# A four-layer graph network in one kernel: the work at the edges between its layers in another order

## The reference

```python
# layer 0
qk = h @ Wqk; q, k = split(qk); v = h @ Wv
w = inv_scale * mask * sum(q * (adj @ (k * mask)), -1)
x = x + softmax(w, axis=1)[:, :, None] * v
# layer 1
query, keyt, value = h @ Wq.T + bq, h @ Wk.T + bk, h @ Wv.T + bv
weight = adj * exp(query @ keyt.T)
x = x + (weight / sum(weight, 2)) @ value
# layer 2: 8 heads of 64
q, k, v = proj(Wq, bq), proj(Wk, bk), proj(Wv, bv)
attn = softmax((q @ k.T) * SCALE * (adj + adj))
x = x + (attn @ v) @ Wo.T + bo
# layer 3: 3 hops
Xw = h @ Wv + bv
e = leaky_relu((Xw @ aw[:d])[:, None, :] + (Xw @ aw[d:])[:, :, None] + ab, 0.2)
T = adj * exp(e) / (sum(adj * exp(e), -1) + 1e-12)
H = h @ Wk[0] + bk[0] + (T @ h) @ Wk[1] + bk[1] + (T @ T @ h) @ Wk[2] + bk[2]
x = x + relu(H)
```

## Time and profile before

| | us |
|---|---|
| time of the kernel, median of 3 runs | 2273.91 (2278.74, 2273.74, 2273.91) |
| the profiled execution, its own time | 2279.19 |
| span of its instructions in the trace | 2277.4 |
| PE busy | 2230.5 (98%) |
| DVE, ACT, POOL busy | 1317.8, 780.9, 722.9 |
| TensorE clock granted, mean | 0.994 of full speed |

### The profile page before, as it was taken

The page is one execution under the profiler, slowest core; times in us unless marked ns, Lnnn a source line. Parts: engine busy times, 40 slices in busy tenths (PEclk is TensorE's granted clock), DMA queues, the critical chain, the costliest instruction groups (busy, mean ns, idle before and its releaser), DMA issues.

```text
span 2277.4 us, 39277 instructions
## 1 busy us (share of the span) xinstructions
PE 2230.5 (98%) x15788; PEld 1767.0 (78%) x15788; DVE 1317.8 (58%) x2643; ACT 780.9 (34%) x1393; POOL 722.9 (32%) x927
## 2 busy tenths in 40 slices
PE   8999999999999999999999999999899999999998
PEld 4788878887887877888888888888677777777776
DVE  3565655656555566455565555564775757575752
ACT  3433333333223233333232333333343434343432
POOL 2433433343334323223332223332341313132320
PEclk9999999999999999999999999999999999999999
DMA  6333333333333343322333323334344242425231
GB/s 204 79 80 99 101 103 84 93 93 84 95 96 107 99 130 108 105 84 80 94 102 98 103 80 83 100 93 110 109 123 127 71 124 68 127 69 128 71 106 37
DMA packets 185687, 224.74 MB, mean 99 GB/s; under 512 B 69408, under 2 KB 85792, under 8 KB 185504
## 3 DMA queue, kind: packets, MB, share of 16 engines
q1 hardware_dynamic: 178832, 212.78, 34.0%
q10 hardware_dynamic: 6672, 9.45, 1.7%
HBM read 88.91 MB, written 50.37 MB: 61 GB/s over the span
## 4 chain that ended last, share of the span: by engine, by line
PE 78%; DVE 8%; SPq 5%; DMA 5%; POOL 1%; issue 1%; ACT 1%; DVEq 0%; ACTq 0%; POOLq 0%
PE bank L316 40%; PE bank L306 29%; SPq L951 5%; DVE junk L933 3%; PE bank L332 3%; DMA x<-mid 2%; PE bank L502 1%; PE bank L567 1%; PE bank L472 1%; PE bank L367 1%; DVE hs L635 1%; DVE stA L610 1%; DMA hGA<-hs 1%; DMA si<-stB 0%; DVE yt L933 0%
## 5 line engine op out<-in xcount | busy, mean ns | idle before, releaser
L316 PE MATMUL bank<-w_hi,h3T_hi 128*128 128x512 f32 x768 | 306.5, 399 | 1.8 <-ACT Z L958 1.8
L316 PE MATMUL bank<-w_lo,h3T_hi 128*128 128x512 f32 x768 | 300.7, 392 | 0.0
L316 PE MATMUL bank<-w_hi,h3T_lo 128*128 128x512 f32 x768 | 300.5, 391 | 0.0
L972 ACT ACTIVATE hn<-x,stA 128x512 f32<-128x512 f32 x192 | 140.7, 804 | 259.8 <-POOL stA L1208 253.9
L1203 POOL TENSOR_SCALAR stA<-stA 128x4 f32<-128x4 f32 x48 | 11.5, 240 | 672.7 <-DVE stA L612 672.5
L610 DVE BATCH_NORM_STATS2 stA<-x 128x6 f32<-128x512 f32 x192 | 128.3, 668 | 160.4 <-DMA x<-mid 151.2
L316 PEld LDWEIGHTS bank<-w_hi,h3T_hi 128*128 128x128 f32 x768 | 144.8, 189 | 56.6 <-issue 25.2
L958 ACT ACTIVATE Z<-bank 64x512 f32<-64x512 f32 x256 | 151.9, 593 | 83.0 <-PE bank L316 67.1
L316 PEld LDWEIGHTS bank<-w_hi,h3T_lo 128*128 128x128 f32 x768 | 145.0, 189 | 30.9
L316 PEld LDWEIGHTS bank<-w_lo,h3T_hi 128*128 128x128 f32 x768 | 144.8, 189 | 29.2
L1216 POOL TENSOR_TENSOR h1T_lo<-hGB,h1T_hi 128x512 fp32r<-128x512 f32 x64 | 81.6, 1304 | 199.2 <-ACT h1T_hi L958 199.2
(11 more groups left out here) (197 smaller groups left out, 5670.7 us busy)
## 6 DMA issues: line engine op xcount, KB each, us to landing
hGA<-hs SPq DMA_DIRECT2D x760, 64.0 KB, 2.0
mid<-x SPq DMA_DIRECT2D x32, 1024.0 KB, 4.5
x<-mid SPq DMA_DIRECT2D x32, 1024.0 KB, 5.9
hGB<-hs SPq DMA_DIRECT2D x256, 64.0 KB, 2.0
x<-in_x SPq DMA_DIRECT2D x15, 1024.0 KB, 5.8
out<-x SPq DMA_DIRECT2D x15, 1024.0 KB, 8.9
blk<-in_adj SPq DMA_DIRECT2D x128, 64.0 KB
PT<-hs SPq DMA_DIRECT2D x120, 64.0 KB, 2.0
```

Source lines behind the costliest of these rows:

```text
L316: ins = eng.matmul(b[:], h[l][:, k, ts], W[r][:, k, :], start=(k == 0 and i == 0), stop=(last and k == 3 and i == 2))
L972: eng.activation(h[t][:], xt[:, t, :], ACT.Relu, bias=st[:, t, 10:11], scale=st[:, t, 9:10]).then_inc(done, 1)
```

## The change

The order of work is changed at four places, and adj is read in another layout:

- **Start.** Layer 0's first operands, the two halves of Wqk, come in four quarters of each instead of two, with a semaphore each, and the first group of x is loaded by SP behind the first two quarters; before, ACT's queue issued it.
- **Layers 0/1 to layer 2.** q2(0) is computed right behind `l01_pv(14)`, ahead of `g1(15)`; ACT splits Wq2 and evicts QQ(0) in that turn. The whole chain of group 1 of layer 2 (statistics, scale, norm, transposes, gather) also goes into that turn; on SP it stands ahead of the load of Wv2.
- **Layer 2 to layer 3.** The row-sum instructions of group 0 (`l3_sums(0)`) go from the last turn with on = true to the one behind it, the transposes of layer 3's group 0 behind the context's lo part; the hi and lo parts of h3T(0) follow.
- **Layer 3.** `l3_rowsum(g)`, for g above 0, goes into group g's own turn, behind two z2 products (for g = 0 behind two z1 products) instead of the turn before; SP's transfers of the sums go behind the gather. The last group's y products and second hop are done by row halves (y 0, y 2, hop; y 1, y 3, hop).
- **Layout.** adj comes in three orders from the host (by rows, by columns, by heads). It needs one DMA for 4 (columns) or 2 for 4 (heads), in rows of 1 KB or more rather than 128 or 256 B, and DVE no longer transposes it (`adj_T`, one instruction per group and layer).

```diff
-                pe.wait_ge((d_qk0, d_qk1)[k // 2], 32)
+                pe.wait_ge(d_qk[k], 32)
...
+                if g == NG:
+                    l2_gemm_T("q2", 0, Wq2, a_q)
...
-                if on:
+                if on and g:
                     l2_gemm_T("q2", g, Wq2, a_q)
...
+            def l3_y(g, t):
+                gemm_open(("y", g, t), hT3[g % 2], t, W3[0], (v_y, 4 * g + (1, 3, 2, 4)[t]), False)
...
                 for t in range(4):
                     gemm(("z2", g, t), hT3[i], t, W3[2], (a_zh[0], 8 * g + 2 * t + 2))
-                    if g == 0 and t == 1:
-                        l3_rowsum(0)
+                    if g and t == 1:
+                        l3_rowsum(g)
                 pe.wait_ge(p_wlo, lo_pool["w1"])
                 for t in range(4):
                     gemm_open(("z1", g, t), hT3[i], t, W3[1], (a_zh[1], 8 * g + 2 * t + 2), False)
+                    if g == 0 and t == 1:
+                        l3_rowsum(0)
                 l3_hop(0, "z1", g)
                 pe.wait_ge(p_wlo, lo_pool["w0"])
-                for t in range(4):
-                    gemm_open(("y", g, t), hT3[i], t, W3[0], (v_y, 4 * g + (1, 3, 2, 4)[t]), False)
-                    if t == 1 + (g == 0) and g + 1 < NG:
-                        l3_rowsum(g + 1)
-                l3_hop(1, "y", g)
+                if g + 1 < NG:
+                    for t in range(4):
+                        l3_y(g, t)
+                    l3_hop(1, "y", g)
+                else:
+                    for r in range(2):
+                        l3_y(g, r)
+                        l3_y(g, 2 + r)
+                        l3_hop(1, "y", g, (r,))
...
                     features2_lo(0)
+                    stats_A(2, 1)
+                    split_in_place(Wk2, "k2")
+                    transposes(2, 1)
                 if on1:
-                    adj_T(0, g - 1)
-                    if g == NG:
...
                 if g == NG:
+                    l3_sums(dve, eng, 0, (0, 1))
                     l2_out(g - 2, 3)
-                stats_A(*(after2(g) if on else (3, 1)))
+                    l3_sums(dve, eng, 0, (2, 3))
+                    l2_out(g - 1, 0)
+                    l2_ctx(g - 1, 1)
+                    stats_A(3, 1)
+                    l2_out(g - 1, 1)
+                    transposes(3, 1)
+                    l3_alpha(0)
+                    l2_out(g - 1, 2)
+                    l3_sums(dve, eng, 1, (0, 1))
+                    l2_out(g - 1, 3)
+                    break
+                if g:
+                    stats_A(*after2(g))
                 if prev:
                     l2_out(g - 1, 0)
-                if on:
+                if on and 0 < g < NG - 1:
                     transposes(*after2(g))
                 if prev:
                     l2_ctx(g - 1, 1)
                 if g == NG - 1:
-                    l3_sums(dve, eng, 0, (0, 1))
+                    transposes(3, 0)
                 for u in range(2):
                     if prev:
                         for t in ((1,), (2,) if g == NG - 1 else (2, 3))[u]:
                             l2_out(g - 1, t)
-                    if on:
-                        l2_softmax(g, u)
-                    elif u == 0:
-                        transposes(3, 1)
-                        adj_T(3, 0)
-                        l3_alpha(0)
-                if not on:
-                    l3_sums(dve, eng, 1, (0, 1))
-                if on:
-                    dve.wait_ge(d_bv2, 16)
-                    if g == NG - 1:
-                        l3_sums(dve, eng, 0, (2, 3))
-                    for t in range(4):
-                        if t == 1:
-                            if g + 1 < NG:
-                                features2_lo(g + 1)
-                                l2_pT(g)
-                        dve.wait_ge(*bank.done(("v2", g, t)))
-                        if g:
-                            dve.wait_ge(*bank.done(("ctx", g - 1, 1, 1)))
-                        eng.tensor_tensor(VV[:, t, :], bank.of(("v2", g, t))[:], bv2, ALU.add).then_inc(v_vv, 1)
+                    l2_softmax(g, u)
+                dve.wait_ge(d_bv2, 16)
+                for t in range(4):
+                    if t == 1 and g + 1 < NG:
+                        features2_lo(g + 1)
+                        l2_pT(g)
+                    dve.wait_ge(*bank.done(("v2", g, t)))
+                    if g:
+                        dve.wait_ge(*bank.done(("ctx", g - 1, 1, 1)))
+                    eng.tensor_tensor(VV[:, t, :], bank.of(("v2", g, t))[:], bv2, ALU.add).then_inc(v_vv, 1)
...
                 if g == 0:
-                    l3_rowsum(0)
                     l3_sums(dve, eng, 1, (2, 3))
+                l3_rowsum(g)
                 if g + 2 < NG:
                     stats_A(3, g + 2)
                 if g + 1 < NG:
-                    adj_T(3, g + 1)
                     l3_alpha(g + 1)
                 if g + 2 < NG:
                     transposes(3, g + 2)
                     l3_sums(dve, eng, g + 2, range(4))
-                if g + 1 < NG:
-                    l3_rowsum(g + 1)
...
-            first = g == 0 and 0 in ts
...
+                    split_in_place(Wq2, d_q2)
                     act.wait_ge(*bank.done(("v1", NG - 2, 3)))
-                    features2_hi(1, NG - 1, hT[1], (0, 1, 2))
-                    split_in_place(Wq2, d_q2)
-                    features2_hi(1, NG - 1, hT[1], (3,))
+                    features2_hi(1, NG - 1, hT[1])
+                    l2_evict("q2", 0, QQ, 0, a_q)
...
-                if on:
+                if on and g:
...
-                if g == 0:
-                    norm_A(*after2(0))
...
-                if on and g:
+                if on and 0 < g < NG - 1:
                     norm_A(*after2(g))
                 if prev:
                     l2_ctx(g - 1, 1)
+                if g == NG - 1:
+                    norm_A(3, 0)
...
+                    l2_exp(g, 1)
                     if g == NG - 1:
                         split_in_place(W3[2], d_w2)
                         split_in_place(W3[1], d_w1)
...
-                elif on:
-                    act.wait_ge(v_dotA, 4)
-                    features2_hi(3, 0, hT3[0])
...
+                    act.wait_ge(v_cst, 1)
+                    features2_hi(3, 0, hT3[0])
...
-                    if g == 0 and t == 1:
-                        l3_T_other(0)
+                l3_T_other(g)
...
-                if g + 1 < NG:
-                    l3_T_other(g + 1)
...
                     scale_A(*((0, g + 1) if g + 1 < NG else (2, 0)))
+                else:
+                    scale_A(2, 1)
+                if on0:
...
+                    split_in_place(W3[2], "w2")
                     features_lo(3, 0, hT3[0], hGA, p_flo3)
-                    split_in_place(W3[2], "w2")
...
+                if g:
+                    l3_rowsum(g)
...
-                    l3_rowsum(g + 1)
...
-                eng.dma_start(abf[:, g % 2], adj_t[g]).then_inc(d_adj[g % 2], 16)
+                eng.dma_start(abf[:, g % 2].rearrange("p t n -> p (t n)"), adj_rows[g]).then_inc(d_adj[g % 2], 16)
...
+            for k in range(4):
+                if k == 2:
+                    load_x(0, x_v[0])
+                eng.dma_start(qT[:, k, :], qk_rows[:, k, :]).then_inc(d_qk[k], 16)
+                eng.dma_start(kTw[:, k, :], qk_rows[:, 4 + k, :]).then_inc(d_qk[k], 16)
...
+            load2(1)
+            gather(2, 1)
             for oc in range(4):
                 sp.wait_ge(*bank.done(("g1", NG - 1, oc)))
             eng.dma_start(Wv2["raw"][:], rows(L2_gnn_Wv)).then_inc(d_v2, 16)
...
-                if on:
+                if on and g:
                     gather(*after2(g))
                 if g == NG:
+                    load_blocks(3, 0)
+                    load3(2)
+                    sums_out3(0)
                     sums_in3(0)
                     gather(3, 1)
-                if g == NG - 1:
-                    sums_out3(0)
...
-            load3(2)
+            sums_out3(1)
+            sums_in3(1)
             for g in range(NG):
                 load_blocks(3, g + 1)
-                if g == 0:
-                    sums_out3(1)
-                sums_in3(g + 1)
-                sums_out3(g + 2)
                 gather(3, g + 2)
                 load3(g + 3)
...
```

120 lines of the change are left out of this document (54 added, 66 removed).

## The result

| | us |
|---|---|
| the kernel before, 5 runs | median 2277.93 (2273.74 to 2282.74) |
| the changed kernel, 5 runs | median 2291.38 (2290.01 to 2293.74) |
| ratio after to before, 95% interval | 1.0063 (1.0044 to 1.0081) |
| the profiled execution after, its own time and span | 2293.74 and 2291.9 (before: 2279.19 and 2277.4) |

A forecast was written before the change was run, and what follows sets the result against it. PE, busy 2230.5 of 2277.4 us, was taken as the bound, with some 47 us idle to change. The terms sum to +3.1: 2282.3 on the profiled execution, 2277.0 carried to the median; range 2264 to 2285 with the rivals.

The forecast's parts named there:

- What would show it: Signs listed for the later profile, such as PE waiting about 12 us on h2T_lo and some 4 us for cT_lo.
- Start, +1.2: Kernel start: g0 stays bound by x and its gather, gains 0.4 from adj, loses 1.6 to low clock; +1.2 us.
- q2(0) first, +7.4: Edge of layers 0/1 to 2: PE waits 11.8 us for h2T_lo(0) in place of 4.4; +7.4 us.
- Group 1's gather ahead of Wv2, +6.1: Same edge: the gather delays Wv2 and x2(15), so k2(0) waits 4.5 us plus 1.6 of clock; +6.1 us.
- Layers 2 to 3, -2.6: Edge of layers 2 and 3: z2(0) starts 4.8 us earlier, 2.2 are given back behind asum(0); -2.6 us.
- Layer 3 later, -7.2: Layer 3's later groups: three row-sum waits of 5.6 us go, with 1.6 of clock; -7.2 us.
- Tail, -1.8: Kernel end: by halves, only four DVE instructions remain behind PE's end instead of eight; -1.8 us.
- The layout, 0: adj's layout: DVE transposes and DMA issues go, all beside a PE that is the bound; 0 us.
- rival B: Slower, at layer 3's start: the list behind asum(0) is too long, -2.6 becomes +3.3, total 2283 us; chance 0.25.

The follow-up runs named there:

- e10: The changed kernel with group 0's x issued by ACT's queue at 0.7 us as before, Wqk still in quarters; ratio 1.0035 to the kernel before.
- e3: The changed kernel with h2T_lo(0) moved ahead of q2w_lo and x2(14) on DVE; ratio 1.0053 to the kernel before.
- e9: The changed kernel with h2T_lo(0) ahead of vf(14)'s first addition, q2w_lo between its second and third, Wv2 ahead of the gather; ratio 0.9967 to the kernel before.
- e2: The changed kernel with the load of Wv2 ahead of group 1's gather on SP; ratio 1.0031 to the kernel before.
- e7: The changed kernel with other orders of ACT and GpSimd in layer 3's first group only; ratio 1.0037 to the kernel before.
- e12: The changed kernel itself, unedited, measured again in a later session; ratio 1.0069 to the kernel before.
- e13: The kernel before with adj's new layout alone, every order as before; ratio 0.998 to the kernel before.
- e16: The kernel before with adj's new layout alone, profiled a second time; layer 3's 13 groups took 486.85 us.
- e6: The changed kernel with x loaded ahead of the gather on SP in layer 3's loop; ratio 1.003 to the kernel before.
- e15: The changed kernel with the last group's y and second hop in one piece, as before; ratio 1.0045 to the kernel before.
- e8: The changed kernel with layer 3's row sums for groups above 0 placed and ordered as before; ratio 1.0043 to the kernel before.

## Why the prediction was wrong

The direction of the sum was right, its size was not: +3.1 forecast, +14.6 in the traces, +13.5 in the medians. The step that failed most is the price of the edge of layers 0/1 and 2: +13.5 forecast for its two terms, +18.6 measured, and of that miss of 5.1 the term for group 1's gather ahead of Wv2 has 4.2 (+10.3 instead of +6.1). The start (+3.9 instead of +1.2) and the edge of layers 2 and 3 (-0.2 instead of -2.6) follow, each 2.4 to 2.7 us off. The waits named under "What would show it" were all seen, so most of the mechanisms were right and their prices too low; the start's premise and the cause of layer 3's waits were wrong. The median on which I put the forecast, 2273.91 of three runs, was also 4.0 us under that of five; measured from 2277.93, the forecast would have been 2281. By its steps:

- **Start, +1.2.** The failed step is "x is asked for no earlier than before (now on SP behind 1 MB of quarters), and the bytes are the same, so 36.4 stays". x left ACT's queue at 0.7 us before; behind the quarters it was asked for at 2.6 and landed at 10.9 instead of 8.7, so g0(0) started at 38.1. That is +1.7, and the low clock, which was forecast, cost 2.2 instead of 1.6 (g0(0) took 13.4 us, 11.2 before). +3.9, and e10 shows that only x's place matters.
- **q2(0) first, +7.4.** Right in mechanism and nearly in size: +8.3, a little over its upper bound of +7.9, since q2w_lo took 5.71, not 4.7, beside POOL's subtraction. e3 and e9 show that DVE's order was the cause.
- **Group 1's gather ahead of Wv2, +6.1.** Right in mechanism, the term was undersized. The chain of 25.4 us from the end of g1(15) was 29.1: Wv2 was taken as 5.3 and took 6.8, 1.5 of it for its own issue; v2w_hi and v2w_lo together were taken as 3.3 and took 5.2, v2w_lo mostly beside POOL. The wait was 7.5 us, and 2.8 were lost at the low clock behind it, more than the 1.6 I had taken for every stall. e2 shows the cause.
- **Layers 2 to 3, -2.6.** -0.2. The cT_lo wait was 4.1, as forecast; but the products behind it lost 3.1 us at 0.52 of the clock, not 1.6. At QK(15) two new waits, 2.4 us, are put down to "issue"; their cause stays open. So z2(0) came 2.2 us earlier and not 4.8. The last part, +2.03 against "2.2 are given back", fitted by luck: the stretch between group 0's hops is 19.5 us in this trace and 20.2 to 23.8 in the eleven others without e7's orders. e7 shows that it is ACT's and GpSimd's lists.
- **Layer 3 later, -7.2.** -5.9 in the first trace, -4.0 in e12's, and the cause was wrong. I had said that the three waits came "from Town standing behind the gather and the sums on SP". e13 and e16 have the old order and one such wait of 1.3 us each; the layout, which I had put at 0, takes the others away. The new order gains nothing on top and costs: the 13 groups take 487.6 and 489.4 us with it, 485.2 and 486.9 with the layout alone. x's load stood behind the gather before too; new is that the write of the sums follows right behind it. Its loads of x took up to 11.6 us to land in the changed kernel, 6.2 to 8.8 with the layout alone, and e6 wins back what that costs.
- **Tail, -1.8.** The tail itself was that, 7.12 to 5.32, but PE's last stretch grew by 0.9, which I had not counted: 0.4 by the halves and 0.5 by group 15's row-sum product (e15, e8).
- **The layout, 0.** Wrong: -4.6 us by e13's ratio of 0.998, outside the bounds of -1 and +0.3.

In rival B, -2.6 and 5.6 more make +3.0 and not +3.3.

Two faults lie behind these. The low clock was taken as 1.6 us behind every stall, and behind the three new ones it was 2.2, 2.8 and 3.1: 3.3 us of the miss. The rows at hand did not show this, since in the longer of the earlier trace rows, 7 us at 0.51 behind VV, PE was busy for only 3.2 of the 7. And I had costed a changed order on SP by what it issues, not by when the loads that move would land.
